# A pair's product with the values, moved to the end of a step and one step nearer to its exponentials (first layer)

## What is computed

```python
q = (hidden_states @ Wq).reshape(b, s, NUM_HEADS, HEAD_DIM)      # 32 heads of 16
kv = hidden_states @ Wkv
k, v = (kv[..., :HEAD_DIM], kv[..., HEAD_DIM:])                  # one k and v for all heads
scores = jnp.einsum('bqhd,bkd->bhqk', q, k) * scale
scores = jnp.where(causal[None, None], scores + bias[None], -jnp.inf)
attn = jax.nn.softmax(scores, axis=-1)
out = jnp.einsum('bhqk,bkd->bqhd', attn, v).reshape(b, s, h)
return out @ Wo
```

## Time and profile before

| | us |
|---|---|
| median of three runs | 2476.23 |
| the profiled execution, its own time | 2481.93 |
| its span, first to last instruction | 2480.1 |
| first layer's pipeline in it, from about 120 to about 720 | 600 |
| TensorE busy in the whole span | 2095.3 (84%) |
| VectorE busy in the whole span | 1771.5 (71%) |
| mean granted TensorE clock | 0.932 of full speed |

### The profile page before, as it was taken

One profiled execution on the slowest core, in us unless ns is written; L12 is line 12 of the kernel. 1 busy time (PEld: TensorE's weight loads), 2 busy tenths in 40 slices (PEclk: granted clock), 3 DMA queues, 4 the chain that ended last, 5 costly groups with the idle time before them and its releaser, 6 DMA issues. The chain is left out here.

```text
span 2480.1 us, 46366 instructions
## 1 busy us (share of the span) xinstructions
PE 2095.3 (84%) x17280; PEld 1245.0 (50%) x17280; DVE 1771.5 (71%) x3733; ACT 1379.1 (56%) x3030; POOL 1004.0 (40%) x927
## 2 busy tenths in 40 slices
PE   7576778778664799999999999999999999667997
PEld 3254555555432455555555555555555556323443
DVE  5487878888754577777777777777777777585554
ACT  3354555555542676766676676666766777251221
POOL 1066676677751333433343334333434343012221
PEclk9798888998786899999999999999999999878999
DMA  5101110101013244334433344344334333410000
GB/s 218 37 13 29 29 32 10 47 13 43 2 35 106 44 82 93 80 65 90 82 73 82 82 90 82 65 90 82 66 84 84 65 67 65 93 58 18 34 17 34
DMA packets 394668, 153.65 MB, mean 62 GB/s; under 512 B 363008, under 2 KB 373888, under 8 KB 392400
## 3 DMA queue, kind: packets, MB, share of 16 engines
q1 hardware_dynamic: 394448, 150.73, 26.7%
HBM read 48.69 MB, written 11.53 MB: 24 GB/s over the span
## 5 line engine op out<-in xcount | busy, mean ns | idle before, releaser
L1434 POOL TENSOR_TENSOR q_in_sbuf<-q_in_sbuf,sinq 128x512 f32<-128x512 f32 x128 | 231.4, 1808 | 688.1 <-ACT q_in_sbuf L1562 581.4
L1574 ACT ACTIVATE xp<-xp,nm 128x128 f32<-128x128 f32 (+3 forms) x512 | 281.3, 550 | 354.2 <-DVE nm L1653 354.2
L784 ACT ACTIVATE weights<-bank,unit 128x512 f32<-128x512 f32 x320 | 210.4, 687 | 272.0 <-PE bank L587 270.8
L1624 DVE SCALAR_TENSOR_TENSOR probs_lo<-xp,rl,probs_hi 128x128 f16<-128x128 f32 (+3 forms) x512 | 263.8, 577 | 109.5 <-ACT probs_hi L1539 109.5
L508 POOL CAST weights_hi<-weights 128x1024 f16<-128x1024 f32 (+1 forms) x192 | 211.1, 1113 | 160.2 <-ACT weights L784 142.6
L1653 DVE CUSTOM_DVE_ANT_0 xp<-bank,mask,cs 128x128 f32<-128x128 f32 (+3 forms) x512 | 250.7, 548 | 0.0
L1539 ACT ACTIVATE probs_hi<-xp,rl 128x128 f16<-128x128 f32 (+3 forms) x512 | 244.0, 549 | 0.7 <-DVE rl L1673 0.7
L1458 PE MATMUL bank<-xT_hi,wq_hi 128*128 128x512 f16 x512 | 196.1, 383 | 46.2 <-DVE yacc L1668 39.0
L1458 PE MATMUL bank<-p1T_hi,v_hi 128*128 128x128 f16 x1280 | 224.7, 221 | 3.1 <-DMA p1T_lo<-probs_lo 3.1
L1458 PE MATMUL bank<-p1T_hi,v_lo 128*128 128x128 f16 x1280 | 224.6, 221 | 0.0
L1458 PE MATMUL bank<-p1T_lo,v_hi 128*128 128x128 f16 x1280 | 224.5, 221 | 0.0
(11 more groups left out here) (307 smaller groups left out, 5732.8 us busy)
## 6 DMA issues: line engine op xcount, KB each, us to landing
raw_q<-in_wq SPq DMA_DIRECT2D x8, 1024.0 KB, 5.4
raw_o<-in_wo SPq DMA_DIRECT2D x8, 1024.0 KB, 5.5
x_front<-in_x SPq DMA_DIRECT2D x4, 1024.0 KB, 5.7
q_stack<-q_hi SPq DMA_DIRECT2D x256, 16.0 KB, 1.8
xb<-in_x SPq DMA_DIRECT2D x4, 1024.0 KB, 5.3
x_before<-x_scratch SPq DMA_DIRECT2D x4, 1024.0 KB, 5.6
wup<-in_wup SPq DMA_DIRECT2D x3, 1024.0 KB, 11.2
fused_scratch<-fused SPq DMA_DIRECT2D x12, 256.0 KB, 2.9
```

Of the source, the lines that this page charges most:

```text
L784: act.activation(px[:, p % 2, i, :], bank_of(("x", p, i))[:, :], ACT.Exp, scale=unit[:, 0:1]).then_inc(s_ed, 1)
L1434: pool.tensor_tensor(qs[:, i % 2, :], qs[:, i % 2, :], rope["sink" if u[0] == "k" else "sinq"][:, :], ALU.mult).then_inc(s_rot, 1)
L1574: ins = act.activation(x, x, ACT.Exp, scale=-1.0, bias=nm[:, m % 3, t:t + 1], accum_out=ls[:, m % 3, t:t + 1])
L1624: ins = dve.scalar_tensor_tensor(pr[1][:, m % 2, c], xp[:, m % 3, c], rl[:, m % 3, t:t + 1], pr[0][:, m % 2, c], ALU.mult, ALU.subtract)
```

## The change

V_LAG goes from 8 to 7, so in step n the product is that of pair n - 7. On TensorE it moves from between turns 1 and 2 to behind turn 4, that is behind everything but the transpose m. In the rotation of the "rest" banks the products follow the other fillings of their step. ScalarE's copy of pair n - 8 now comes behind its first exponential of step n, no longer behind its third; VectorE's reciprocals stay where they were.

```diff
-        X_LAG, V_LAG, N_LAG = 6, 8, 9
+        X_LAG, V_LAG, N_LAG = 6, 7, 9
...
+            fillings["rest"] += others(n)
             if 0 <= n - V_LAG < NP:
                 fillings["rest"].append(("pv", n - V_LAG))
-            fillings["rest"] += others(n)
...
-                    turn(n, 0, 1)
-                    if 0 <= n - V_LAG < NP:
-                        weigh_values(n - V_LAG)
-                    turn(n, 2)
+                    turn(n, 0, 1, 2)
...
                     turn(n, 4)
+                    if 0 <= n - V_LAG < NP:
+                        weigh_values(n - V_LAG)
                     if n % GP == 0 and 0 <= n // GP - 1 < NG:
                         turn_maxima(n // GP - 1)
...
-                        if i == 2 and 0 <= n - V_LAG < NP:
-                            copy_heads(n - V_LAG)
+                        if i == 0 and 0 <= n - V_LAG - 1 < NP:
+                            copy_heads(n - V_LAG - 1)
...
-                    if 0 <= n - V_LAG < NP:
-                        sum_reciprocals(n - V_LAG)
+                    if 0 <= n - V_LAG - 1 < NP:
+                        sum_reciprocals(n - V_LAG - 1)
```

## The result

The changed kernel took 2503.97 us, the median of four runs (2499.2 to 2505.56), against 2476.48 for the kernel before, whose median is now that of four runs too. The ratio is 1.011, with a 95% interval of 1.0089 to 1.0131: 22 to 32 us slower, 27.5 by the medians. The forecast was 2517, its range 2494 to 2551.

What follows compares the result with a forecast made beforehand. It took a loop of waits between engines, through VectorE's `weights_lo` and TensorE's product, as the bound. Order 31.6, gates -7 and clock 16 made 41 us more on 2476: 2517 us, range 2494 to 2551.

Steps and rivals of the forecast that it cites:

- The signs that the prediction named: First layer: product waits near 2.5 us, more score waits, gate waits under 25 us, clock below 0.88, pipeline 40 us longer.
- The gates: TensorE's waits at gates: the product now runs inside them and gives back its time at six or seven, -7 us.
- ScalarE, GpSimd: Earlier copy on ScalarE, bank rotation and GpSimd's casts: no gain or loss counted.
- The clock: TensorE behind longer product waits: half clock for 3.4 us each, between 0 and 42 us, taken as 16 us.
- Where it costs: Steps on TensorE: turns 0 and 1 now stand behind a waiting product, 31.6 us in all.
- The 1.08 us: Turns 0 and 1 on TensorE, now behind the waiting product: each such step's loop comes 1.08 us later.
- the count of 30 products: Products charged the full delay: 24 that waited before and six that newly wait, 32.4 us.
- the price in steps without a q filling: Steps without fillings: VectorE's next `maximise` waits some 0.9 us for scores behind the product.
- The order's cost alone: Rival: longer waits don't lower the clock on TensorE's loop; 24.6 us more, 2501 us; chance 0.25.
- Every longer wait costs its half-clock stretch: Rival: full clock cost on TensorE and no cover by VectorE's other work; 74 us more, 2550 us; chance 0.17.
- Faster: Rival: product costs no wait, frees GpSimd's `weights` buffers sooner and fills the gates; -18 us, 2458 us; chance 0.07.
- No difference: Rival: gates and layernorm statistics swallow every delay; within 5 us, 2476 us; chance 0.06.

Runs made afterwards that it cites:

- e4: Kernel before, with the product between turns 0 and 1 of its step instead of between turns 1 and 2: 2487.17 us, ratio 1.004.
- e6: Changed kernel with 24 matmuls without use ahead of the wait of 47 products: 2487.0 us, ratio to the kernel before 1.0035.
- e1: Kernel before, with only the 15 products of gate steps moved to the end of the step before: 2486.14 us, ratio 1.0034.
- e2: Kernel before, with every product except those of gate steps moved ahead, behind any transpose m; old rotation and copies: 2500.33 us, ratio 1.0091.
- e3: Kernel before, with all products moved as in the change but behind transpose m; old bank rotation and copies: 2512.89 us, ratio 1.0146.
- e11: Changed kernel with the gate steps' products left between turns 1 and 2 of the gate step: 2496.4 us, ratio to the kernel before 1.0079.
- e5: Changed kernel with ScalarE's copy back behind the third exponential: 2515.19 us, ratio to the kernel before 1.0151.
- e9: Kernel before, with all products moved behind transpose m and the copy behind the first exponential; old bank rotation: 2517.64 us, ratio 1.015.
- e7: Kernel before, with 14 matmuls without use ahead of the wait of 26 products: 2478.0 us, ratio 0.9999.
- e8: Kernel before, with the product moved to just ahead of turn 4 in steps with at most one other filling; V_LAG 8: 2458.94 us, ratio 0.9929.
- e12: Kernel before, with the product later in all steps, behind the first other filling where there are two or three; V_LAG 8: 2477.6 us, ratio 0.9999.
- e10: Changed kernel with V_LAG 8 and N_LAG 10, so the product comes one step later: 2497.82 us, ratio to the kernel before 1.007.

## Why the prediction was right, and where not

*The direction and its place: right.* The loop runs second half of `weights_lo`, product, turns, filling, next half. The product starts 0.1 us behind the half as before, its wait grew by 1.09 us (2.51 against 1.42), and e4 and e6 give 0.54 and 1.06 us for one and two turns. The signs that the prediction named came, but for the size of the whole; that of the clock says little, since over 120 to 760 us it was 0.87 already before.

*The sum, 41 us against 27.5: of its terms the clock's held, the gates' and the order's were off, and one was missing.* The errors go in both directions, so that the sum lies as near as it does is partly luck.

- "The gates": -7 us was forecast. They cost 8 to 13 us (e1, e2 with e3, e11). The prediction took the product's 1 us off the wait at six or seven gates. But the product did not fill the gate's wait with its own time alone: at all 15 it brought a wait of its own, 1.0 to 3.0 us in e1 where it had been 0 to 1.0, for a bank or for `weights_lo`, with two turns behind it. (The reading of the earlier trace rows as ten gates was off by one as well: the longest of the ten waits, 9.5 us, is that of step 6, which has no product.)
- "ScalarE, GpSimd": nothing was forecast for the copy and the rotation. Together they give back 9 to 10 us (e3, e5, e9). The working asked only whether the new rotation does harm. The kernel before had 16.5 us of waits of line 619 for `m_lo`, in a row that the prediction does not use; in the order of the change 9 to 10 us of them would be left (e3, e9), and the companions remove nearly all. (The copy's "0.4 us earlier" stands in no row; it moves ahead of two exponentials.)
- "The clock": 16 us was forecast, and the filler shows 17 to 19, known to some 6 us (e6), and a control of nothing (e7). This term stood, though its size had been picked from a range of 0 to 42. The upper bound, 42 us, was too high: 37 of 43 longer waits were followed by a low clock, but not all of that time lay on the loop. The mean clock hides the term: it went from 0.87 to 0.86 over 120 to 760 us.
- "Where it costs": 31.6 us for the order of product and turns, outside the gates. e2, which moved just these products, cost 23 us with the clock's part in it, against a forecast of 31.6 and the clock's 16. Another estimate: the change with filler is 9 us slower than before, and with the 9 to 10 of the companions put back that leaves some 18 us for order and gates together without the clock, where 31.6 - 7 = 24.6 was forecast. It holds if the filler gave back all of the clock's cost; either way it is good to a few us only, and how the 18 divide between gates and the rest is not shown. The 1.08 us is confirmed in steps with a q filling. What was too high is so the count of 30 products, or the price in steps without a q filling; no run tells the two apart.

*The rivals.* "The order's cost alone", 2501 us, is nearest to the measured time, but its reason is refuted: the clock does cost. That it came close is luck: the clock's 17 us and the gates' wrong sign, some 15 to 20 us too little, were nearly made up by the order's cost put too high and the unseen gain of the companions. "Every longer wait costs its half-clock stretch", 2550 us, has the mechanism of the clock right and its size at twice what e6 gives. "Faster" was right that the gates' waits shrink (40.6 to 15.6 us) and wrong that this gives time. "No difference" is excluded by the interval.

*Left open.* Why e8 gains 18 us and not at most 12; the clock is a candidate, and no run takes it apart. What e12 loses it by. Whether the end of the step with the old lag is slow by itself: e10 mixed it with a later `norm_heads`.

## What to carry to other kernels

Work that sits inside an engine's wait is free as long as it brings no wait of its own, and an instruction that waits should have as much independent work ahead of it as its releaser leaves time for; before pulling a waiting instruction forward, look at when its releaser ends, not at when its own input was begun. Count what a longer wait does to the clock of what follows it on the loop, and check that with idle-time filler and a control, since the mean clock hardly moves. When a ring of buffers changes its order, list the waits that it removes as well as those that it may add: here they were a third of the result.

## What the runs showed of the hardware that was not expected

Matmuls whose results are thrown away made a kernel faster by 17 us of 2504. They filled waits of mostly 2.0 to 3.3 us, and the clock over the first layer rose from 0.86 to 0.90. A smaller dose in the kernel before, at 26 products whose waits were mostly 0.9 to 1.6 us (17 of them), raised it from 0.87 to 0.89 and changed the time by nothing that could be measured. In the kernel before a wait of 1.42 us was followed by full clock; in the change one of 2.51 us was followed by 0.53. That is the common case in each kernel and not a limit: 6 of the 43 waits of 2.0 to 3.3 us in the change were followed by full clock, and 2 of the 22 of 0.9 to 1.6 us in the kernel before by a low one.
